# Attention in float32: the row maxima turned by ScalarE and VectorE, and the key blocks of the softmax sum dealt out anew

## The reference, cut to what matters

```python
h = _layernorm(x, axis=-1) * (1 + ca) + sa
q = (h @ wq_w + wq_b).reshape(bs, sl, 32, 32)
k = (h @ wk_w + wk_b).reshape(bs, sl, 8, 32)
v = (h @ wv_w + wv_b).reshape(bs, sl, 8, 32)
qg = q.reshape(bs, sl, 8, 4, 32)
attn = einsum('bqhfd,bkhd->bhfqk', qg, k) / sqrt(32)
att = softmax(attn, axis=-1)
a = einsum('bhfqk,bkhd->bqhfd', att, v).reshape(bs, sl, 1024)
x = x + ga * (a @ wo_w + wo_b)
```

## Time and profile before

| | |
|---|---|
| time, median of 3 runs | 2799.31 us (2798.43 to 2799.71) |
| the profiled execution | 2796.36 us, span 2794.5 us |
| TensorE matmuls | 2750.2 us busy, 98% |
| VectorE | 2178.0 us busy, 78% |
| GpSimd | 1906.9 us busy, 68% |
| ScalarE | 1529.6 us busy, 55% |

### The profile page before, as it was taken

One profiled execution on the slowest core, in us unless ns is written; L12 is line 12 of the kernel. 1 busy time (PEld: TensorE's weight loads), 2 busy tenths in 40 slices (PEclk: granted clock), 3 DMA queues, 4 the chain that ended last, 5 costly groups with the idle time before them and its releaser, 6 DMA issues.

```text
span 2794.5 us, 49051 instructions
## 1 busy us (share of the span) xinstructions
PE 2750.2 (98%) x14654; PEld 1696.9 (61%) x14654; DVE 2178.0 (78%) x2809; ACT 1529.6 (55%) x3023; POOL 1906.9 (68%) x710
## 2 busy tenths in 40 slices
PE   7999999999999999999999999999999998999998
PEld 4788888884444444444444444444444447888887
DVE  4433334348999999999999999999999958676667
ACT  3211111116777776767777777767776763455454
POOL 2433333317999999999999999999999986111110
PEclk9999999999999999999999999999999999999999
DMA  7544443434444434344344344443444443323332
GB/s 267 182 144 137 147 137 135 135 114 133 92 88 99 91 87 100 85 87 100 85 92 95 85 98 89 91 98 84 96 93 87 99 132 102 114 96 108 113 100 81
DMA packets 167644, 307.05 MB, mean 110 GB/s; under 512 B 50000, under 2 KB 91408, under 8 KB 159504
## 3 DMA queue, kind: packets, MB, share of 16 engines
q1 hardware_dynamic: 158496, 240.05, 29.5%
q0 software_dynamic: 9072, 66.06, 11.6%
HBM read 159.12 MB, written 79.82 MB: 86 GB/s over the span
## 4 chain that ended last, share of the span: by engine, by line
PE 71%; POOL 3%; DVE 2%; issue 1%; ACT 0%; POOLq 0%; DVEq 0%; ACTq 0%
PE back_ps L1354 20%; PE back_ps L1368 17%; PE s_ps L1328 16%; PE s_ps L1944 12%; POOL p_sum L1129 3%; PE back_ps L1993 2%; PE back_ps L1385 2%; PE back_ps L2012 1%; PE back_ps L1965 1%; DVE mx L1243 0%; PE back_ps L1343 0%; ACT h_t L1725 0%; DVE xn L1799 0%; DVE two_sum L1258 0%; PE back_ps L2019 0%
## 5 line engine op out<-in xcount | busy, mean ns | idle before, releaser
L1223 ACT ACTIVATE p_t<-back_ps 128x512 f32<-128x512 f32 x2048 | 1114.6, 596 | 426.6 <-PE back_ps L1354 388.2
L1243 DVE TENSOR_REDUCE mx<-s_ps 128x1 f32<-128x1024 f32 x1002 | 1172.0, 1208 | 81.9 <-PE s_ps L1328 73.9
L1129 POOL TENSOR_TENSOR p_sum<-p_sum,p_t 128x2048 f32<-128x2048 f32 x254 | 1166.9, 4594 | 22.0 <-ACT p_t L1223 5.7
L1354 PE MATMUL back_ps<-q_st,k_st 98*128 98x512 f32 x2048 | 806.2, 434 | 4.2 <-POOL ones L1098 2.4
L1354 PEld LDWEIGHTS back_ps<-q_st,k_st 98*128 98x128 f32 x2048 | 343.9, 187 | 582.2 <-ACT p_t L1223 483.7
L1328 PE MATMUL s_ps<-k_st,q_st 96*128 96x512 f32 x2004 | 634.3, 397 | 0.7 <-DVE mx L1243 0.4
L1368 PE MATMUL back_ps<-p_t,v_sb 128*32 128x512 f32 x4096 | 546.4, 605 | 0.0
L1328 PEld LDWEIGHTS s_ps<-k_st,q_st 96*128 96x128 f32 x2004 | 379.3, 189 | 77.7 <-DVE mx L1243 8.8
L1258 DVE TENSOR_REDUCE two_sum<-p_t 128x512 f32<-128x1024 f32 x256 | 317.5, 1242 | 8.7 <-DMA p_sum<-two_sum 8.7
L574 POOL TENSOR_TENSOR o_lo<-side,o_hi 128x512 fp32r<-128x512 f32 x80 | 104.3, 1304 | 320.8 <-ACT o_hi L544 320.7
L1129 POOL TENSOR_TENSOR p_sum<-p_t 128x2048 f32<-128x2048 f32 x64 | 313.0, 4891 | 9.3 <-ACT p_t L1223 9.3
(11 more groups left out here) (186 smaller groups left out, 2917.9 us busy)
## 6 DMA issues: line engine op xcount, KB each, us to landing
p_sum<-two_sum POOLq DMA_DIRECT2D x63, 1024.0 KB, 6.9
q_st<-q_hi_d SPq DMA_DIRECT2D x128, 256.0 KB, 4.4
stage<-w_mod SPq DMA_DIRECT2D x48, 512.0 KB, 6.4
q_hi_d<-o_hi SPq DMA_DIRECT2D x64, 256.0 KB, 2.0
q_lo_d<-o_lo SPq DMA_DIRECT2D x64, 256.0 KB, 2.1
q_st<-q_lo_d SPq DMA_DIRECT2D x64, 256.0 KB, 4.1
att_d<-a_sb SPq DMA_DIRECT2D x128, 128.0 KB, 2.3
a_f<-att_d SPq DMA_DIRECT2D x32, 512.0 KB, 4.7
```

Source lines behind the costliest of these rows:

```text
L1129: nc.gpsimd.tensor_tensor(total, before, p_t[:, kt, :, :], ALU.add).then_inc(sum_done, 1)
L1223: nc.scalar.activation(p_t[:, s, c, :], st_ps[:, c % 2, :], ACT.Exp, scale=SCALE)\
L1243: nc.vector.tensor_reduce(mx[:, slot % 2, e:e + 1], s_ps[:, e % 2, :], AX_X, ALU.max)\
L1354: nc.tensor.matmul(st_ps[:, c % 2, :], k_st[:, slot // 2, s * P:(s + 1) * P], q_st[:, slot, jj, h * QW:(h + 1) * QW], start=True, stop=True)\
```

## The change

It does five things.

- The turn of the maxima leaves TensorE. ScalarE copies the 16 columns of maxima of a pair, rounded to float32r, into m_parts[:, 0:16] and negates them back into a second half of mx; VectorE adds the two halves of mx (maximum less its high part: the low part) into m_parts[:, 16:32], and transposes m_parts in blocks of 32x32 into m_rows. Both stand at the place of m_lo, in step 6. k_st now holds -1.0 in the two rows.
- m_rows has the 32x32 blocks one over the other, so four transfers (`put_rows`) in place of two write the rows of q_st.
- VectorE adds blocks 2 and 3 instead of 3 and 4, and only half of their tiles (HALF), in steps 4 and 5 instead of 5, 6, 7 and 0.
- GpSimd adds blocks 0 and 1, the other half of 2 and 3 in two half-size adds, and 4 and 5; it adds VectorE's half sums in a further half-size add, at the start of the next pair.
- Blocks 6 and 7 are added by transfers: `merge` adds block 6 of p_t onto block 7 when all numerators of the pair are done, and `join`, which waits for it, adds block 7 onto p_sum. ScalarE waits for `merged` before it writes block 6 again, and for `joined` before block 7.

The last pair is handled on its own, as before (its blocks 6 and 7 go to `add_two` on TensorE). The core of the diff:

```diff
+def put_rows(sp, q_st, slot, m_rows, landed):
+    rows = q_st[96:98, slot, :, :].bitcast(F32).rearrange("h j (t b r) -> h b (j t) r", b=4, r=32)
+    for b in range(4):
+        sp.dma_start(rows[:, b, :, :], m_rows[32 * b:32 * b + 32, slot % 2, :]).then_inc(landed, 16)
...
         def put_max(pair, slot):
-            sp.wait_ge(m_lo_done, pair + 1)
-            for n, part in enumerate((m_hi, m_lo)):
-                sp.dma_start(q_st[STACK + n:STACK + n + 1, slot, :, :].bitcast(F32)
-                             .rearrange("o j s -> o (j s)"), part[:, :].bitcast(F32))\
-                  .then_inc(m_in, 16)
+            sp.wait_ge(m_turned, pair + 1)
+            put_rows(sp, q_st, slot, m_rows, m_in)
...
+        def merge(pair):
+            pool.wait_ge(num_done, pair * STEPS + STEPS)
+            pool.sem_inc(waited_pool, 1)
+            nc.gpsimd.dma_start(p_t[:, LATE[1], :, :].rearrange("p c q -> p (c q)"),
+                                p_t[:, LATE[0], :, :].rearrange("p c q -> p (c q)"), accum_op=ALU.add)\
+              .then_inc(merged, 16)
+
         def join(pair, par):
+            pool.wait_ge(merged, pair * 16 + 16)
             pool.wait_ge(sum_done, pair * SUMS + SUMS)
-            pool.wait_ge(two_done, pair * REP + REP)
             pool.sem_inc(waited_pool, 1)
             nc.gpsimd.dma_start(p_sum[:, par, :, :].rearrange("p c q -> p (c q)"),
-                                two_sum[:, :, :].rearrange("p c q -> p (c q)"), accum_op=ALU.add)\
+                                p_t[:, LATE[1], :, :].rearrange("p c q -> p (c q)"), accum_op=ALU.add)\
               .then_inc(joined, 16)
+
+        def add_half(pair, par):
+            half = p_sum[:, par, 0:HALF, :]
+            pool.wait_ge(two_done, pair * HALF + HALF)
+            pool.wait_ge(sum_done, pair * SUMS + 5)
+            nc.gpsimd.tensor_tensor(half, half, two_sum[:, 0:HALF, :], ALU.add).then_inc(sum_done, 1)
 
         def do(pair, slot, it):
             if not below(pair, 1):
+                merge(pair - 1)
+                add_half(pair - 1, (slot - 1) % 2)
+            total = p_sum[:, slot % 2, :, :]
+            pool.wait_ge(exp_done, pair * TILES + 2 * REP)
...
+            nc.gpsimd.tensor_tensor(total, p_t[:, 0, :, :], p_t[:, 1, :, :], ALU.add).then_inc(sum_done, 1)
+            if not below(pair, 1):
                 join(pair - 1, (slot - 1) % 2)
...
+            if not is_int(pair, NPAIR - 1):
+                for kt in (TWO, TWO + 1):
+                    pool.wait_ge(exp_done, pair * TILES + (kt + 1) * REP)
+                    pool.wait_ge(sum_done, pair * SUMS + made)
+                    nc.gpsimd.tensor_tensor(total[:, HALF:REP, :], total[:, HALF:REP, :], p_t[:, kt, HALF:REP, :], ALU.add)\
+                      .then_inc(sum_done, 1)
+                    made += 1
+            if not below(pair, 2):
+                divide(pair - 2, slot % 2)
+            for kt in (4, 5):
...
+        def max_hi(pair, slot):
+            act.wait_ge(max_done, pair * NS + NS)
...
+            nc.scalar.copy(m_parts[:, slot % 2, 0:NS], mx[:, slot % 2, 0, :]).then_inc(m_hi_done, 1)
+            act.wait_ge(m_hi_done, pair + 1)
+            nc.scalar.activation(mx[:, slot % 2, 1, :], m_parts[:, slot % 2, 0:NS].bitcast(F32), ACT.Copy, scale=-1.0)\
+              .then_inc(m_back_done, 1)
...
+        def max_lo(pair, slot):
+            dve.wait_ge(m_back_done, pair + 1)
+            nc.vector.tensor_reduce(m_parts[:, slot % 2, NS:2 * NS].bitcast(F32),
+                                    mx[:, slot % 2, :, :].rearrange("p s e -> p e s"), AX_X, ALU.add)\
+              .then_inc(m_lo_done, 1)
+
+        def turn_max(pair, slot):
+            dve.wait_ge(m_lo_done, pair + 1)
+            if not below(pair, 2):
+                dve.wait_ge(m_in, pair * 64 - 64)
+            nc.vector.transpose(m_rows[:, slot % 2, :], m_parts[:, slot % 2, :].bitcast(F32)).then_inc(m_turned, 1)
...
-                if s == TURN_STEP + 1 and not is_int(pair, NPAIR - 1):
-                    max_lo(pair + 1)
-                if s == 0 and not below(pair, 1):
-                    add_two(pair - 1, REP - 1)
+                if s == MAX_STEP + 1 and not is_int(pair, NPAIR - 1):
+                    max_lo(pair + 1, slot + 1)
+                    turn_max(pair + 1, slot + 1)
                 if s in TWO_STEPS:
                     add_two(pair, TWO_STEPS.index(s))
```

with these constants:

```diff
-    ADDED = (0, 1, 2, 5, 6, 7)
-    SUMS = len(ADDED) - 1
+    SUMS = 6
+    USED_AT = {0: 1, 1: 1, 2: 2, 3: 3, 4: 4, 5: 5}
     LATE = (6, 7)
-    TWO = 3
-    TWO_STEPS = (5, 6, 7)
+    TWO = 2
+    HALF = REP // 2
+    TWO_STEPS = (4, 5)
```

## The result

The change makes the kernel slightly slower: 2805.81 us (median of 10 runs, 2802.01 to 2810.91) against 2799.28 (10 runs, 2797.22 to 2802.51), a ratio of 1.0024 with a 95% interval of 1.0016 to 1.0032. The profiled execution took 2806.28 us.

A forecast was written before the change was run, and what follows sets the result against it. TensorE's order of work was taken as the clock. VectorE stalls +25.5, rows +2.0, turn -12.6, GpSimd -1.7 and pair 0 -1.0 gave +12.2 on 2796.36: 2808.6 profiled, 2811 median; range 2783 to 2832 us.

The forecast's parts named there:

- the rows: SyncE, each pair's end: four row transfers instead of two land barely in time for the next score; 0.03 a pair, +2 us.
- pair 0: First pair: today's three stretched steps, about 0.3 each, go away; -1.0 us.
- VectorE's burst: Steps 5 and 6: additions beside maxima make VectorE late; TensorE stalls 0.23 or, with a w_o piece, 0.58 a pair; +25.5 us.
- The limit of +1.84 for VectorE: In each step VectorE must be free 1.84 us after its start; anything beyond lengthens the step one for one.
- the rival with VectorE in time: Step 6: no stall, as TensorE's limit lies later or VectorE is quicker; 2784 us, chance 0.21.
- The forecast's point at which turn and stall cancel: At a mean stall of 0.25 a pair the two cancel; result within 0.2% (2794 to 2805), chance 0.14.
- The turn: TensorE, once per pair: 63 turns of the maxima by 0.20 removed from the chain, -12.6 us.
- ScalarE: Two small instructions replace one copy before the exponentials; 0.55 and a handshake hidden in 0.82 of idle time, no charge.
- The rival of late rows: Small transfers land 0.5 later or issue slower; 62 pairs each wait 0.5 more at the first score: 2840, chance 0.14.
- GpSimd: Its cycle falls to 25.1, below TensorE's 25.9 to 26.3, so it stops pushing; at most 0.06 in 28 waits, -1.7 us.
- the rival of a loop: GpSimd with its transfers: landings over about 9 us make it and ScalarE's block 7 late; over 2850 at 10, chance 0.04.
- I charge nothing: Start and last two pairs: GpSimd's full adds end as before within 1 us, so no time is added.

The follow-up runs named there:

- moved_4_7: Changed kernel with VectorE's two additions in steps 4 and 7 and the w_o split in step 5, last pair's additions unmoved: 2774.82 us, 0.9920 of before.
- split_step6: Changed kernel with only VectorE's split of the w_o piece moved from step 4 to step 6: 2794.52 us, 0.9989 of before.
- sums_5_7: Changed kernel with the maxima turned by TensorE as before, VectorE's additions in steps 5 and 7, w_o split in step 4: 2792.95 us, 0.9980 of before.
- rows_late: Changed kernel with additions in steps 4 and 7, split in step 5, plus a 4 KB transfer ahead of the four row transfers: 2793.46 us, 0.9987 of before.
- pad_128B: Changed kernel with the freed 128 bytes per partition left empty, so later buffers lie as before the change: 2810.02 us, 1.0041 of before.
- before_low: Kernel before with mx moved to the end of SBUF, so later buffers lie 128 bytes lower: 2791.51 us, 0.9983 of before.
- max_only: Changed kernel keeping the new turn of the maxima, with the sums of the kernel before: 2799.12 us, 1.0004 of before.
- pad_64B: Changed kernel with 64 bytes per partition left empty behind the rows of the maxima: 2817.42 us, 1.0074 of before.

## Why the prediction was right

The mechanism, its place and its size were as forecast: 2811 predicted, 2805.81 measured. Of the smaller terms the rows and pair 0 were off, and one was missing. Point by point:

**VectorE's burst: right.** Forecast 0.23 in step 6 of the even pairs, measured 0.25 (3.35); forecast 0.25 and 0.33 in steps 5 and 6 of the pairs with a piece of w_o, measured 0.24 and 0.33 (3.34 and 3.43). In the odd pair shown VectorE is free for step 5 at T = 17.61 and for step 6 at T = 21.03 (1413.62 and 1417.04 less 1396.01), where the forecast had 17.61 and 21.04. 30 x 0.25 + 32 x 0.57 = 25.7 us against 25.5. moved_4_7 and split_step6 show that it is this: without neighbours the stall is zero, with the piece moved away each pair keeps only the stall that the even ones had. Odd pairs are 0.29 longer than even ones (26.36 and 26.07), and not 0.35. The limit of +1.84 for VectorE, read from two rows, held; the rival with VectorE in time is what moved_4_7 made of it. The forecast's point at which turn and stall cancel (a mean stall of 0.25) is nearly split_step6, with a mean of 0.24: its time to the last denominator is 685.4 + 1561.9 + 58.4 against 685.1 + 1557.5 + 59.4, +3.7 us, where the last stage then gives 4.8 back. It cancels with the place of the buffers and not quite without it.

**Pair 0: 1.0 forecast, about 0.2 given.** The row is the first step of pair 1, where VectorE still has pair 0's last addition; the three stretched steps are step 7 of pair 0 (3.42) and steps 0 and 1 of pair 1 (3.40 and 3.46), 0.98 over 3.10, and in the kernel after the last two are 3.10. But step 7 of pair 0 has no denominator to cover the rows of the maxima, and it grows to 3.90 (657.97 to 661.87). The chain that ended last goes there through SyncE's four issues (the fourth at 659.13) and 1.75 us of the transfer. The forecast charged the rows of this pair 0.03 like those of any other; what it measured is 0.80 over 3.10.

**The turn: right.** Step 5 of the even pairs is 3.10, where the earlier trace rows had 3.30. Between sums_5_7 and moved_4_7 the turn is worth 0.167 a pair, a little less than 0.20, though step 5 alone differs by the full 0.20.

**ScalarE: right.** The two small instructions stand in a gap, timeline of ACT of the kernel after:

```profile
1412.15 0.20 ACT L1218 CAST m_parts<-mx 128x16 fp32r<-128x16 f32 x1
1412.38 0.22 ACT L1220 ACTIVATE mx<-m_parts 128x16 f32<-128x16 f32 x1
1413.08 1.09 ACT L1263 ACTIVATE p_t<-back_ps 128x512 f32<-128x512 f32 x2 [0.49 <-PE back_ps L1394]
```

The exponentials behind them still wait 0.49 for TensorE. On VectorE the small sum takes 0.19 and the transpose 0.21, where I took 0.2 each with no row to go by; that these came out is luck.

**The rows: too small.** I charged 0.03 a pair. Timeline of SP, which answers to the earlier trace rows:

```profile
1417.60 2.71 SPq L57 DMA_DIRECT2D q_st<-m_rows  x4
```

The four issues begin at 1417.60, 1418.33, 1419.05 and 1419.70, 0.70 apart as in the mean of all pairs, and not 0.63; the load that waits for the fourth starts at 1421.50, 1.80 later. The landing is therefore the 1.8 of the earlier trace rows, and the issue is slower. Step 7 is 4.07 to 4.08 against 4.02: 0.05 to 0.06 a pair, some 3.4 us and not 2.0. (The forecast's own sum of this path, 21.63 + 3 x 0.63 + 1.8, is 25.32 and not 25.35; the charge of 0.03 doesn't rest on so fine a difference.) The Trainium skill, page "DMA: Bandwidth & Descriptors", section "Why small descriptors are slow (HBM only)", says that transfers between SBUF and SBUF don't suffer the penalty of small descriptors, and this trace agrees for a transfer of 4 KB: in pieces of 128 bytes it landed no later than one of 8 KB in pieces of 512. The rival of late rows charged a late row one for one. rows_late bears this out beyond a cover: 0.61 more at the issue costs 0.32 of wait, since with VectorE in time 0.29 is covered. That the kernel after, whose maxima come late, has no such cover follows from its 55 waits; no run delays its rows.

**GpSimd: right.** Timeline of POOL of the kernel after, which answers to the earlier trace rows, and the DMA issues of its page (KB, us to landing), which answer to the earlier trace rows:

```profile
1424.08 0.87 POOL L1117 DMA_DIRECT2D p_t<-p_t  x1 [1.53 <-PE back_ps L1408]
1424.69 2.69 POOL L1136 TENSOR_TENSOR p_sum<-p_sum,two_sum 128x1024 f32<-128x1024 f32 x1
...
1428.21 4.58 POOL L1147 TENSOR_TENSOR p_sum<-p_t 128x2048 f32<-128x2048 f32 x1 [0.83 <-ACT p_t L1263]
```

```profile
p_t<-p_t POOLq DMA_DIRECT2D x63, 1024.0 KB, 8.4
p_sum<-p_t POOLq DMA_DIRECT2D x63, 1024.0 KB, 7.0
```

GpSimd waits 1.53 and 0.83 in a cycle: it has slack and pushes nothing. Its push before is visible in step 7, 4.03 in the mean before and 4.01 to 4.02 in sums_5_7: some 1 us over the pairs, where 1.7 was forecast. The first transfer takes 8.4 to land, longer than the 6.9 of the earlier trace rows. It is issued at T = 1.7, so it lands at T = 10.1 in the median, at the late end of the forecast 8 to 10; the rival of a loop asked for a landing of more than 9 us, which only single ones take (9.5 at most). The second is issued at T = 10.8 and lands 7.0 later, at T = 17.7 (forecast 18.4). No exponential waits for a transfer. The half add costs 2.55 in the mean and 2.69 beside the transfer, not 2.35; it is hidden.

**The last stage: a term that the forecast did not have.** Its "I charge nothing" is said of the start and the last two pairs, where 0.9 came out; the last stage isn't in the sum at all. It gave 4.5 us back, and pad_128B and before_low show that this follows the place to which the freed 128 bytes moved its buffers. Against the profiled execution: forecast +12.2, measured +14.4 to the last denominator (15.4 in the 60 pairs, -0.1 ahead, -0.9 behind) and -4.5 after it, +9.9. Of the 2.2 too much in the first, 1.4 are the rows and 0.8 is pair 0, as an estimate: the time to the first denominator alone repeats within 3 us only. The median of the runs then lies 0.5 below the profiled execution and not 2.95 above it, which is most of the 5.2 us between forecast and result. So the burst was foreseen for good reasons. The closeness of the total is in part luck: what was too low for the rows and pair 0 and what was missing for the last stage have opposite signs.

## What to carry to other kernels

When one engine feeds another through a double buffer, what counts is the work between two hand-overs, not the total: VectorE lost 131 us and the kernel got slower, because two additions stood in neighbouring steps. The same additions two or three steps apart took 28.5 us off the 60 pairs of the changed kernel, which are then 13 us shorter than before; the rest of moved_4_7's 0.8% is the place of the buffers and the spread of the stages around. A small instruction on the bounding engine can be a respite for its supplier: in the even pairs the stall is 0.04 with the turn and 0.25 without it, and in max_only the turn gave 0.20 a pair while its removal and 0.25 more work on VectorE cost 0.45. So spread the supplier's work first. And when a change frees or takes a few bytes of SBUF, time a version with the bytes padded back before crediting the change with what other stages do.

## What the runs showed of the hardware that was not expected

The pace of 512-column float32r matmuls depends on where buffers lie in SBUF, here most likely w_o, the only one of their operands that moved. A shift of the later buffers by 128 bytes per partition changes the mean distance of two starts from 0.2327 to 0.2280 us (means of one 400 to 396 and 395 to 390 ns), 4 to 5 us of a stage of 490 in two profiles set side by side and 6.5 in the mean of all, forwards in before_low and back in pad_128B; with a shift by 64 bytes it is 0.2302, and the first stage is slower too, 2817.42 us in all. The mean granted clock was 0.996 in the profiled executions of the changed kernel and of before_low, and 0.995 in that of pad_64B, which is too little to explain 9 us in one stage of 685. What rule the addresses follow stays open.
